# The last attention round in two halves, and ranks of tokens summed by TensorE

## The chip, the cores and the metric

The program runs on one core of one Trainium2 chip. The metric is the device time of one execution in microseconds, as the median of several. Engines: TensorE (PE; its weight loads are listed as PEld), VectorE (DVE), ScalarE (ACT), GpSimd (POOL), and SyncE (SP), which issues loads.

## The reference

Three layers over x, 64 batches of 32 tokens of 256 numbers (2048 tokens, 16 tiles of 128):

```python
x = x + _L0_xattn_ref(ctx_1024, ctx_1024, _layernorm(x), ...)   # attention to 257 context rows per batch
x = x + _L0_attn_ref(_layernorm(x), w_qkv, w_gate, w_out)       # causal linear attention, 16 heads of 64
x = x + _L0_ffn_ref(_layernorm(x), gate_w, w1, w2, w3)          # 8 experts, each token goes to 2

# linear attention
q = jax.nn.elu(q) + 1.0
k = jax.nn.elu(k) + 1.0
k_cum = jnp.cumsum(k, axis=1)
kv = jnp.cumsum(k[..., None, :] * v[..., :, None], axis=1)
numerator = jnp.einsum('bthj,bthij->bthi', q, kv)
denominator = jnp.einsum('bthj,bthj->bth', q, k_cum)
out = numerator / (denominator[..., None] + 1e-06) * gate

# experts
scores = xt @ gate_w.T
top_vals, top_idx = jax.lax.top_k(scores, TOP_K)
top_w = jax.nn.softmax(top_vals, axis=-1)
h = jax.nn.silu(xt @ w1[e].T) * (xt @ w3[e].T);  y = combine * (h @ w2[e].T)
```

## The kernel before

The kernel has four stages. First comes the cross attention, one tile of 128 tokens at a time (`xstep`). Then the linear attention runs in `NR` = 8 rounds of two tiles (`astep`, rounds 0 to 7), written as a pipeline: round r computes q, k, gates and values of its own two tiles and finishes the round before. The two tiles of a round are its halves, s = 0 and 1. Third is the routing: every token chooses two experts, and gets a place in a table of 39 tiles of 128 slots, ordered by expert. Last come the 39 expert tiles (`fstep`), with TensorE busy throughout.

In a round, `a_scores` (L728) makes the scores of a half as 32x32 blocks, 64 matmuls of 64x32. `masks` (L1376) multiplies them on VectorE into `att`, for both halves at once. `a_dens` (L745) sums them into denominators, `den_ev` (L1072) copies these on ScalarE, `recip` (L1393) takes reciprocals on VectorE in pieces of 256, and `norm_att` (L1398) multiplies. `a_nums` (L757) makes the numerators in banks 4 to 7 of PSUM; `gated` (L1405) multiplies by the gates into `goT`; `gated_hi` (L1067, ScalarE) and `gated_lo` (L1415, VectorE) split the result for the three-part product; `a_proj` (`mm3`, L536 to L538) does the output projection, 24 matmuls a half, in bank 6, and `x2` (L1421) adds it to `x_all`. Every engine runs its instructions strictly in the order of its program, and waits on counters (semaphores) stand in front of them.

With the last round (r = 7) the pipeline has to be emptied. `drain` does it, one function on each engine. The finished rounds 0 to 7 are also normalised for the experts (`g_stats`, `g_lns` on VectorE with `g_sqrt` on ScalarE), transposed by TensorE (`g_trs`, L813), copied by ScalarE (`g_xT_ev`, L1096) and multiplied with the gate weights (`g_logits`, L823). Of the logits VectorE takes the two best experts of each token (`top_two`, in three parts: tiles 0 to 5, 6 to 11, 12 to 15), and marks them in `chosen` and, both together, in `both` (128 x 16 tiles x 8 experts). The place of a token within its expert is the number of marks ahead of it. Over the tiles this is a running sum on VectorE in `scan` (`counts`, four doubling steps over the first 12 tiles, and four single steps behind the last part). Within a tile it is a product with a strictly triangular matrix; `ranks` (L833 to L835) does both in three matmuls. VectorE reads their result first in `places` (L1523). `warm(n)` (L829) is n matmuls of 256 columns whose result nobody reads; `warm(6)` stands ahead of `ranks` and `warm(20)` behind it. In the table of slots, TensorE's 32 matmuls of L886 follow, as soon as `in_slot` is there.

SyncE loads the weights of the experts (8 of 2 MB) once the gates and values of round 7 are done. The loads keep the DMA full until shortly before 429 us.

Of the kernel before, what the change touches and what calls it, by code (L numbers as in the profile page):

```python
# [104 lines left out]
def build(nc, ctx, a, out):  # L105
# [116 lines left out]
    scan = [nc.alloc_sbuf_tensor_at(f"scan{i}", [P, NT + 8, E], F32, offset=at["low"] + i * 4 * (NT + 8) * E) for i in range(2)]  # L222
# [15 lines left out]
    LOGIT_BANK = (2, 3, 4)  # L238
# [18 lines left out]
    both = place("both", [P, NT, E])  # L257
# [43 lines left out]
    def sem(name):  # L301
# [29 lines left out]
        "part", "var", "sq", "rs", "ln", "tr", "xT", "mm", "sc", "max", "idx", "keep"))  # L331
    r_step, r_d, r_e1, r_both, r_rank, r_id, r_what, r_in, r_rows, r_tab, r_map, r_done, r_w = (
# [200 lines left out]
    def _(pe):  # L533
# [186 lines left out]
        def a_scores(r, s):  # L720
            wait(pe, a_qku, 8 * r + 8)
            wait(pe, a_o, 8 * r)
            for c in range(FC):
                for b in range(BT):
                    tok = slice(s * P + b * T, s * P + (b + 1) * T)
                    for h in range(2):
                        rows = slice(h * HD, (h + 1) * HD)
                        m = pe.matmul(ps[b * T:(b + 1) * T, 4 + h, (s * FC + c) * T:(s * FC + c + 1) * T],  # L728
                                      kT[rows, c, tok], qT[rows, c, tok], start=True, stop=True,
                                      tile_position=(h * HD, b * T))  # L730
            if s == 1:
                m.then_inc(a_sc, 1)
# [9 lines left out]
        def a_dens(r):  # L742
            wait(pe, a_att, 2 * r + 2)
            for s in range(2):
                pe.matmul(ps[:, 4 + s, :], con[:, C_TWOS:C_TWOS + P], att[:, s, :, :, :].rearrange("p c h t -> p (c h t)"),  # L745
                          start=True, stop=True).then_inc(a_den, 1)

        def a_nums(r, s):
            wait(pe, a_norm, 2 * r + s + 1)
            wait(pe, a_x2, r)  # L750
            wait(pe, a_vu, 4 * r + 4)
            wait(pe, a_o, 8 * r + 4 * s)
            for c in range(FC):
                for h in range(2):
                    for b in range(BT):
                        rows = slice(b * T, (b + 1) * T)
                        m = pe.matmul(ps[h * HD:(h + 1) * HD, 4 + b, (s * FC + c) * T:(s * FC + c + 1) * T],  # L757
                                      v_sb[rows, s, (2 * c + h) * HD:(2 * c + h + 1) * HD], att[rows, s, c, h, :],
                                      start=True, stop=True, tile_position=(b * T, h * HD))
            m.then_inc(a_num, 1)  # L760

        def a_proj(r, u, s, cs=range(FC)):
            wait(pe, a_o, 8 * r + 8)
# [3 lines left out]
            for c in cs:  # L767
                m = mm3(ps[:, 6, s * D:(s + 1) * D], goh[:, c, rows], gol[:, u, c, rows], w_out_hi[:, c, :], w_out_lo[:, c, :],
                        c == 0, c == FC - 1)
# [3 lines left out]
        def astep(r, u):  # L773
# [9 lines left out]
            if r == NR - 1:  # L783
# [5 lines left out]
                a_values(r, 1, range(1, 2))  # L789
                a_gates(r, range(3, 4))  # L790
# [16 lines left out]
        def g_trs(r):  # L807
            wait(pe, g_ln, 2 * r + 2)
            wait(pe, a_gtu, 2 * NT)
            wait(pe, g_xT, r - 1)  # L810
# [6 lines left out]
        def g_logits(r):  # L817
            wait(pe, g_xT, r + 1)
            bank = LOGIT_BANK[part_of(2 * r)]
# [11 lines left out]
        def ranks():  # L831
            pe.wait_ge(r_both, 1)
            pe.matmul(ps[:, 0, 0:NT * E], con[:, C_LOW:C_LOW + P], both[:, :, :].rearrange("p t e -> p (t e)"), start=True, stop=False)  # L833
            pe.matmul(ps[:, 0, 0:NT * E], ones, scan[0][:, 7:7 + NT, :].rearrange("p t e -> p (t e)"), start=False, stop=True)
            pe.matmul(ps[:, 1, 0:E], ones, scan[0][:, 7 + NT, :], start=True, stop=True).then_inc(r_rank, 1)  # L835

        def drain(r, u):
            a_proj(r - 1, 1 - u, 0, range(0, FC // 2))
            a_dens(r)
            a_proj(r - 1, 1 - u, 0, range(FC // 2, FC))  # L840
            a_proj(r - 1, 1 - u, 1)
            g_trs(0)
            g_trs(1)
            g_logits(0)
            a_nums(r, 0)
            g_trs(2)
            g_logits(1)
# [14 lines left out]
            warm(6)  # L862
            ranks()
# [97 lines left out]
    def _(act):  # L961
# [107 lines left out]
        def den_ev(r):  # L1069
            for s in range(2):  # L1070
                wait(act, a_den, 2 * r + s + 1)
                act.activation(den[:, s, :], ps[:, 4 + s, :], ACT.Identity, bias=con[:, C_EPS2:C_EPS2 + 1]).then_inc(a_de, 1)  # L1072
# [25 lines left out]
        def astep(r, u):  # L1098
            before = valid(r - 1, NR)
            if before:  # L1100
                elu_parts(r, range(0, 4))
                den_ev(r - 1)
# [6 lines left out]
            if r == NR - 1:  # L1109
                gates(r, u, range(3, 4))  # L1110
# [7 lines left out]
        def drain(r, u):  # L1118
            den_ev(r)
            for k in range(3):  # L1120
                g_xT_ev(k)
            gated_hi(r, u, 0)
            gated_hi(r, u, 1)
            g_xT_ev(3)
            g_sqrt(r - 1)
            g_xT_ev(4)
            g_xT_ev(5)
# [104 lines left out]
    def _(dve):  # L1232
# [145 lines left out]

        def elu(r, n):
# [38 lines left out]
        def x2(r):  # L1418
            rows = x_all[:, bass.ds(2 * r, 2), :].rearrange("p a d -> p (a d)")
            wait(dve, a_y, r + 1)  # L1420
            dve.tensor_tensor(rows, ps[:, 6, :], rows, ALU.add).then_inc(a_x2, 1)  # L1421
# [30 lines left out]
        def astep(r, u):  # L1452
# [20 lines left out]
            if before:  # L1473
                for s in range(2):
                    gated(r - 1, 1 - u, s)
                    gated_lo(r - 1, 1 - u, s)
# [19 lines left out]
        def top_two(part):  # L1496
            ts = slice(*PARTS[part])
# [18 lines left out]
            link(dve.tensor_tensor(both[:, ts, :], by_k[:, :, 0, :], by_k[:, :, 1, :], ALU.add))  # L1516

        def places():
            dve.wait_ge(r_rank, 1)
            seen = ps[:, 0, 0:NT * E].rearrange("p (t e) -> p t e", e=E)  # L1520
# [20 lines left out]
        def counts():  # L1541
            for b in scan:
                link(dve.memset(b[:, 0:8, :], 0.0))
            link(dve.tensor_copy(scan[0][:, 8:8 + LATE_T, :], both[:, 0:LATE_T, :]))
            cur = 0
            for d in (1, 2, 4, 8):
                link(dve.tensor_tensor(scan[1 - cur][:, 8:8 + LATE_T, :], scan[cur][:, 8:8 + LATE_T, :],
                                       scan[cur][:, 8 - d:8 - d + LATE_T, :], ALU.add))
                cur = 1 - cur
            assert cur == 0  # L1550
# [57 lines left out]
        for t in range(LATE_T, NT - 1):  # L1608
            link(dve.tensor_tensor(scan[0][:, 8 + t, :], scan[0][:, 7 + t, :], both[:, t, :], ALU.add))
        dve.tensor_tensor(scan[0][:, 7 + NT, :], scan[0][:, 6 + NT, :], both[:, NT - 1, :], ALU.add).then_inc(r_both, 1)  # L1610
# [8 lines left out]
        link(dve.tensor_tensor(cmp[:, :, :], ps[:, 1, 0:E].rearrange("p (e a) -> p e a", a=1).to_broadcast([P, E, MAXT]),  # L1619
# [140 lines left out]
```

## Time and profile before

| | us |
|---|---|
| median of 3 runs | 834.27 |
| lowest, highest | 832.51, 835.47 |
| the profiled execution | 833.98 |
| its span in the trace | 832.1 |
| TensorE busy in the span | 796.2 (96%) |
| VectorE busy | 637.9 (77%) |
| ScalarE busy | 564.5 (68%) |
| mean granted TensorE clock | 0.981 |

Times in the trace count from the start of the span. A granted clock of 1.00 is 2.4 GHz, of 0.50 1.2 GHz. The cross attention ends near 105 us, the rounds near 385, and the expert tiles begin at 446.5. The records of successive matmuls overlap, so the distance between two starts tells the pace, not the length of one record. An idle time in brackets is that of the engine just before the row, with what released it.

### The profile page before, as it was taken

The numbers are of one execution on the slowest core, as the hardware profiler recorded it, in microseconds if no ns is written. First come the engines' busy times: TensorE is split into PE (matmuls) and PEld (weight loads), VectorE is DVE, ScalarE is ACT, GpSimd is POOL, SyncE is SP. The second block draws the span as 40 slices with busy tenths as digits, with TensorE's granted clock in tenths as the row PEclk, the third lists the DMA queues.
The fourth block names the chain that finished last, engine by engine and source line by source line (L and its number), as shares of the span: only waits on it lengthen the run. The fifth ranks groups of instructions, "written<-read, shape, count | busy, mean of one in ns | idle before, by whom it ended". The sixth has DMA issues, their size and how long they took to land.

```text
span 832.1 us, 24093 instructions
## 1 busy us (share of the span) xinstructions
PE 796.2 (96%) x9270; PEld 695.7 (84%) x9270; DVE 637.9 (77%) x1033; ACT 564.5 (68%) x879; POOL 281.5 (34%) x190
## 2 busy tenths in 40 slices
PE   6899999999999999999898999999999999999993
PEld 4566588998999999997886889888898888998883
DVE  4444543756758485676679999999999999999992
ACT  3545456554646656463147999989998999999971
POOL 0333375020220202010001545555564555555531
PEclk9999999999999999999689999999999999999997
DMA  9999920000000000005962455445555455544552
GB/s 350 416 417 414 387 79 2 2 16 16 15 28 3 28 2 28 17 15 212 423 241 69 137 147 145 134 126 140 144 147 136 126 137 146 148 136 126 135 143 37
DMA packets 31771, 115.92 MB, mean 139 GB/s; under 512 B 4465, under 2 KB 11570, under 8 KB 26578
## 3 DMA queue, kind: packets, MB, share of 16 engines
q1 hardware_dynamic: 22834, 100.17, 33.5%
q0 software_dynamic: 8864, 14.69, 8.3%
q8 instruction: 57, 0.93, 0.5%
q14 instruction: 16, 0.13, 0.0%
HBM read 105.27 MB, written 9.57 MB: 138 GB/s over the span
## 4 chain that ended last, share of the span: by engine, by line
PE 89%; DVE 4%; DMA 3%; issue 2%; ACT 1%; POOL 0%; POOLq 0%; SPq 0%; DVEq 0%; ACTq 0%
PE ps L536 23%; PE ps L538 22%; PE ps L537 22%; PE ps L941 4%; PE ps L757 3%; PE ps L728 2%; PE ps L589 2%; PE ps L646 2%; PE ps L601 2%; PE ps L623 1%; DMA ctx_t<-in_ctxT 1%; PE ps L904 1%; PE ps L620 1%; PE ps L829 1%; PE ps L823 1%
## 5 line engine op out<-in xcount | busy, mean ns | idle before, releaser
L1599 DVE TENSOR_TENSOR w_lo<-w,w_hi 128x1024 fp32r<-128x1024 f32 x156 | 186.5, 1217 | 0.1
L1163 ACT ACTIVATE w_hi<-w 128x1024 fp32r x156 | 161.3, 1061 | 2.8 <-DVE tile_e L1657 2.8
L522 POOL DMA_INDIRECT out_x<-y_sb,slot_row x39 | 122.5, 3142 | 119.1 <-ACT y_sb L1195 119.1
L536 PE MATMUL ps<-w_hi,xh 128*128 128x512 f32 x312 | 125.7, 403 | 0.4 <-DVE xl L1693 0.4
L538 PE MATMUL ps<-w_hi,xl 128*128 128x512 f32 x312 | 121.9, 391 | 0.0
L537 PE MATMUL ps<-w_lo,xh 128*128 128x512 f32 x312 | 121.6, 390 | 0.0
L536 PE MATMUL ps<-xT_hi,wa_hi 128*128 128x256 f32 x384 | 109.3, 285 | 1.0 <-ACT v_sb L1085 0.8
L537 PE MATMUL ps<-xT_lo,wa_hi 128*128 128x256 f32 x384 | 107.8, 281 | 0.0
L538 PE MATMUL ps<-xT_hi,wa_lo 128*128 128x256 f32 x384 | 107.8, 281 | 0.0
L1174 ACT ACTIVATE w_hi<-w_sb 128x1024 fp32r<-128x1024 f32 x78 | 82.7, 1061 | 29.9 <-DMA w_sb<-in_w 18.3
L510 POOL DMA_INDIRECT xs_sb<-xn_d,slot_row x39 | 68.1, 1746 | 95.9 <-PE ps L904 74.0
L536 PE MATMUL ps<-w_hi,hh 128*128 128x256 f32 x312 | 92.1, 295 | 2.9 <-DVE hl L1700 2.9
L1679 DVE TENSOR_TENSOR w_lo<-w_sb,w_hi 128x1024 fp32r<-128x1024 f32 x78 | 91.8, 1217 | 2.1 <-ACT w_hi L1174 2.1
L538 PE MATMUL ps<-w_hi,hl 128*128 128x256 f32 x312 | 88.8, 285 | 0.0
L537 PE MATMUL ps<-w_lo,hh 128*128 128x256 f32 x312 | 88.7, 284 | 0.0
L536 PEld LDWEIGHTS ps<-xT_hi,wa_hi 128*128 128x128 f32 x384 | 72.3, 188 | 2.2 <-issue 1.2
L537 PEld LDWEIGHTS ps<-xT_lo,wa_hi 128*128 128x128 f32 x384 | 72.4, 188 | 0.4
L538 PEld LDWEIGHTS ps<-xT_hi,wa_lo 128*128 128x128 f32 x384 | 72.3, 188 | 0.0
L1053 ACT ACTIVATE neg<-ps 128x512 f32<-128x512 f32 x64 | 38.2, 597 | 46.9 <-PE ps L538 46.9
L538 PEld LDWEIGHTS ps<-w_hi,xl 128*128 128x128 f32 x312 | 58.6, 188 | 12.8
L536 PEld LDWEIGHTS ps<-w_hi,xh 128*128 128x128 f32 x312 | 58.5, 188 | 12.0 <-DVE xl L1693 0.8
L537 PEld LDWEIGHTS ps<-w_lo,xh 128*128 128x128 f32 x312 | 58.6, 188 | 11.1
(219 smaller groups left out, 1761.4 us busy)
## 6 DMA issues: line engine op xcount, KB each, us to landing
w_sb<-in_w SPq DMA_DIRECT2D x78, 512.0 KB
ctx_t<-in_ctxT SPq DMA_DIRECT2D x16, 1028.0 KB, 8.8
ctx_n<-in_ctxN SPq DMA_DIRECT2D x16, 1024.0 KB
w<-in_w SPq DMA_DIRECT2D x8, 2048.0 KB, 14.3
stage<-in_w_a SPq DMA_DIRECT2D x16, 256.0 KB, 8.5
x_all<-in_x SPq DMA_DIRECT2D x4, 512.0 KB, 8.0
out_x<-x_all POOLq DMA_DIRECT2D x8, 256.0 KB, 3.1
xn_d<-xn_first POOLq DMA_DIRECT2D x6, 256.0 KB, 2.8
```

The source lines that it names most:

```text
L510: pool.indirect_dma_start(xs_sb[:, :], None, xn_d, bass.IndirectOffsetOnAxis(slot_row[:, t:t + 1], 0)).then_inc(f_xs, 16)
L522: pool.indirect_dma_start(out, bass.IndirectOffsetOnAxis(slot_row[:, t:t + 1], 0), y_sb[:, :], None, compute_op=ALU.add).then_inc(f_st, 16)
L536: pe.matmul(dst, l_hi, r_hi, start=first, stop=False)
L537: pe.matmul(dst, l_hi, r_lo, start=False, stop=False)
L538: return pe.matmul(dst, l_lo, r_hi, start=False, stop=last)
L757: m = pe.matmul(ps[h * HD:(h + 1) * HD, 4 + b, (s * FC + c) * T:(s * FC + c + 1) * T], v_sb[rows, s, (2 * c + h) * HD:(2 * c + h + 1) * HD ...
L941: m = pe.transpose(ps[:, 4 + c // 4, (c % 4) * P:(c % 4 + 1) * P], h_sb[:, c * P:(c + 1) * P], ident)
L1053: act.activation(neg[:, n % 2, :], ps[:, n % 4, :], ACT.Relu, scale=-1.0).then_inc(a_neg, 1)
L1163: act.activation(w_hi[:, c, :].rearrange("p (c n) -> p c n", c=DC), w13[:, bass.ds(e, 1), c % 2, :, c // 2 * 512:(c // 2 + 1) * 512].rearr ...
L1174: act.activation(w_hi[:, 4 + c, :], src, ACT.Copy).then_inc(f_dhi, 1)
L1599: dve.tensor_tensor(w_lo[:, c, :].rearrange("p (c n) -> p c n", c=DC), w13[:, bass.ds(e, 1), c % 2, :, c // 2 * 512:(c // 2 + 1) * 512].re ...
L1679: dve.tensor_tensor(w_lo[:, 4 + c, :], src, w_hi[:, 4 + c, :].bitcast(F32), ALU.subtract).then_inc(f_dlo, 1)
```

## The change

It has two parts, both in the emptying of the pipeline. In round 7 every step that took both halves now takes one: masks, densities and their copies. The densities and masks of half 0 move forward, among the gates and values of the round. The numerators of half 0 now stand ahead of the projection of round 6. The densities use banks 0 and 1, the projection of rounds 6 and 7 goes to bank 2, and the logits to banks 3, 6 and 4.

In the routing `scan` and `counts` are gone. `both` has one more tile of zeros. TensorE adds the marks of tile t to all later tiles by products of a matrix of ones with `both`, shifted by d = 1 to 16 tiles, accumulated in bank 7: `ranks_most` for the first 12 tiles after the last logits, `ranks_last` for the last four. Only two `warm` matmuls remain ahead. The last column of eight holds the totals of the experts. `top_two(0)` on VectorE moves behind the statistics of round 7.

```diff
         def a_scores(r, s):
             wait(pe, a_qku, 8 * r + 8)
             wait(pe, a_o, 8 * r)
+            if r == NR - 1 and s == 1:
+                pe.wait_ge(a_att, 2 * r + 2)
...
-            if s == 1:
+            if s == 1 or r == NR - 1:
                 m.then_inc(a_sc, 1)
...
-        def a_dens(r):
-            wait(pe, a_att, 2 * r + 2)
-            for s in range(2):
-                pe.matmul(ps[:, 4 + s, :], con[:, C_TWOS:C_TWOS + P], att[:, s, :, :, :].rearrange("p c h t -> p (c h t)"),
-                          start=True, stop=True).then_inc(a_den, 1)
+        def a_dens(r, s):
+            wait(pe, a_att, 2 * r + 2 * s + 2)
+            wait(pe, a_vu, 4 * r + 2)
+            pe.matmul(ps[:, s, :], con[:, C_TWOS:C_TWOS + P], att[:, s, :, :, :].rearrange("p c h t -> p (c h t)"),
+                      start=True, stop=True).then_inc(a_den, 1)
 
         def a_nums(r, s):
             wait(pe, a_norm, 2 * r + s + 1)
-            wait(pe, a_x2, r)
+            wait(pe, a_x2, r if r < NR - 1 else r - 1)
+            if r == NR - 1:
+                pe.wait_ge(a_att, 2 * r + 4)
...
                 a_values(r, 1, range(1, 2))
+                a_dens(r, 0)
                 a_gates(r, range(3, 4))
                 a_scores(r, 1)
...
+        def summed(d, lo, hi):
+            last = min(NT + 1, hi + d)
+            return pe.matmul(ps[:, 7, (lo + d) * E:last * E], ones, both[:, lo:last - d, :].rearrange("p t e -> p (t e)"),
+                             start=False, stop=hi == NT and d == NT - lo, skip_group_check=True)
+
+        def ranks_most():
+            pe.wait_ge(r_both, 2)
+            pe.matmul(ps[:, 7, 0:(NT + 1) * E], con[:, C_LOW:C_LOW + P], both[:, :, :].rearrange("p t e -> p (t e)"),
+                      start=True, stop=False, skip_group_check=True).then_inc(r_low, 1)
+            for d in range(1, NT + 1):
+                summed(d, 0, LATE_T)
+
+        def ranks_last():
+            pe.wait_ge(r_both, 3)
+            pe.matmul(ps[:, 7, LATE_T * E:NT * E], con[:, C_LOW:C_LOW + P], both[:, LATE_T:NT, :].rearrange("p t e -> p (t e)"),
+                      start=False, stop=False, skip_group_check=True)
+            for d in range(1, NT - LATE_T + 1):
+                m = summed(d, LATE_T, NT)
+            m.then_inc(r_rank, 1)
 
         def drain(r, u):
-            a_proj(r - 1, 1 - u, 0, range(0, FC // 2))
-            a_dens(r)
-            a_proj(r - 1, 1 - u, 0, range(FC // 2, FC))
+            a_dens(r, 1)
+            a_nums(r, 0)
+            a_proj(r - 1, 1 - u, 0)
             a_proj(r - 1, 1 - u, 1)
+            a_nums(r, 1)
             g_trs(0)
             g_trs(1)
+            a_proj(r, u, 0)
             g_logits(0)
-            a_nums(r, 0)
             g_trs(2)
+            a_proj(r, u, 1)
             g_logits(1)
-            a_nums(r, 1)
             g_trs(3)
             g_logits(2)
-            a_proj(r, u, 0)
-            a_proj(r, u, 1)
+            g_trs(4)
             g_logits(3)
-            g_trs(4)
             g_trs(5)
...
-            warm(6)
-            ranks()
+            ranks_most()
+            warm(2)
+            ranks_last()
             warm(20)
...
+        def masks_half(r, s):
+            mask = con[:, C_MASK:C_MASK + T].rearrange("p (a t) -> p a t", a=1).to_broadcast([P, FC, T])
+            wait(dve, a_sc, r + s + 1)
...
-        def counts():
-            for b in scan:
-                link(dve.memset(b[:, 0:8, :], 0.0))
-            link(dve.tensor_copy(scan[0][:, 8:8 + LATE_T, :], both[:, 0:LATE_T, :]))
...
         def drain(r, u):
-            masks(r)
-            g_lns(r - 2)
             recip(r, 0)
             recip(r, 1)
-            x2(r - 1)
             norm_att(r, 0)
+            masks_half(r, 1)
+            g_lns(r - 2)
             recip(r, 2)
             recip(r, 3)
             norm_att(r, 1)
             gated(r, u, 0)
+            x2(r - 1)
             gated_lo(r, u, 0)
             gated(r, u, 1)
             gated_lo(r, u, 1)
             g_stats(r - 1)
-            top_two(0)
             g_lns(r - 1)
             x2(r)
             g_stats(r)
+            top_two(0)
             g_lns(r)
             top_two(1)
-            counts()
+            no_tiles()
```

The order of the instructions on TensorE after the last logits, before:

```order
1960 L823 MATMUL ps<-gw,xT_122 128x8 x4
1961 L829 MATMUL ps<-con 128x256 x6
1962 L833 MATMUL ps<-both,con 128x128
1963 L834 MATMUL ps<-scan_126,con 128x128
1964 L835 MATMUL ps<-scan_126,con 128x8
1965 L829 MATMUL ps<-con 128x256 x20
```

and of the changed kernel, where L850 is the line of `summed` and L846 that of `warm`:

```order
1962 L840 MATMUL ps<-gw,xT_122 128x8 x4
1963 L855 MATMUL ps<-both,con 128x136
1964 L850 MATMUL ps<-both,con 128x96 x5
1965 L850 MATMUL ps<-both,con 128x88
...
1975 L850 MATMUL ps<-both,con 128x8
1976 L846 MATMUL ps<-con 128x256 x2
1977 L862 MATMUL ps<-both,con 128x32
1978 L850 MATMUL ps<-both,con 128x32
1979 L850 MATMUL ps<-both,con 128x24
1980 L850 MATMUL ps<-both,con 128x16
1981 L850 MATMUL ps<-both,con 128x8
1982 L846 MATMUL ps<-con 128x256 x20
```

Three matmuls have become 17 ahead of the two `warm` and five behind them.

VectorE at the end of round 7 and the start of `drain`, before (goT is `gated` of round 6, att<-ps,con the masks, den the reciprocals):

```order
376 L1405 SCALAR_TENSOR_TENSOR goT<-goT,ps 128x8x32 x4
377 L1415 TENSOR_TENSOR gol<-goT,goh 128x4x128 x2
378 L1238 BN_STATS bn_2_52<-x_all 128x6 x2
...
385 L1376 TENSOR_TENSOR att<-ps,con 128x16x32 x2
386 L1445 RECIPROCAL rstd_135<-rstd_135 128x2
387 L1449 TENSOR_SCALAR xn_first<-x_all,mean_131,rstd_135 128x256 x2
388 L1393 RECIPROCAL den<-den 128x256 x2
389 L1421 TENSOR_TENSOR x_all<-ps,x_all 128x512
390 L1398 TENSOR_TENSOR att<-att,den 128x512
```

and of the changed kernel:

```order
376 L1445 SCALAR_TENSOR_TENSOR goT<-goT,ps 128x8x32 x4
377 L1416 TENSOR_TENSOR att<-ps,con 128x8x32 x2
378 L1455 TENSOR_TENSOR gol<-goT,goh 128x4x128 x2
379 L1271 BN_STATS bn_2_52<-x_all 128x6 x2
...
386 L1433 RECIPROCAL den<-den 128x256 x2
387 L1438 TENSOR_TENSOR att<-att,den 128x512
388 L1416 TENSOR_TENSOR att<-ps,con 128x8x32 x2
389 L1485 RECIPROCAL rstd_133<-rstd_133 128x2
390 L1489 TENSOR_SCALAR xn_first<-x_all,mean_129,rstd_133 128x256 x2
391 L1433 RECIPROCAL den<-den 128x256 x2
```

The masks of half 0 have moved up behind `gated`, and those of half 1 stand behind two reciprocals and the normalisation of half 0.

## Rows read from the trace of the kernel before

**Rows 1.** Stages: length, busy time of PE, PEld, DVE, ACT, POOL; PEclk, DMA share, GB/s

```profile
392.80:397.40 4.60, 4.35 (x155) 4.05 (x153) 4.36 (x4) 1.26 (x3) 0.71 (x1) 1.00 1.03 439
397.40:406.30 8.90, 5.66 (x146) 5.40 (x146) 5.15 (x13) 2.46 (x5) 0.00 (x0) 0.50 0.99 420
406.30:411.10 4.80, 4.80 (x23) 4.80 (x24) 4.53 (x32) 1.04 (x3) 0.00 (x0) 0.51 1.03 434
411.10:414.10 3.00, 3.00 (x28) 3.00 (x27) 0.99 (x4) 0.00 (x0) 0.71 (x1) 1.00 1.02 426
414.10:421.30 7.20, 6.26 (x56) 5.79 (x54) 5.41 (x35) 3.01 (x6) 1.43 (x2) 1.00 0.99 364
421.30:428.10 6.80, 6.80 (x21) 5.72 (x22) 4.76 (x34) 0.95 (x2) 0.00 (x0) 0.50 1.00 419
```

**Rows 2.** Timeline, 377 to 392: start, length, engine, line, work, idle before

```profile
377.56 1.33 PE L728 MATMUL ps<-qT,kT 64*32 64x32 f32 x128
380.72 0.16 DVE L1439 TENSOR_SCALAR mean<-mean 128x2 f32<-128x2 f32 x1
381.27 0.36 PE L536 MATMUL ps<-xT_hi,wa_hi 128*128 128x256 f32 x1 [0.78 <-ACT v_sb L1085]
385.07 0.28 PE L728 MATMUL ps<-qT,kT 64*32 64x32 f32 x11 [0.97 <-issue]
385.42 1.29 DVE L1376 TENSOR_TENSOR att<-ps,con 128x512 f32<-128x512 f32 x2 [4.54 <-PE ps L728]
386.80 1.95 PE L745 MATMUL ps<-att,con 128*128 128x512 f32 x4
388.65 3.37 DVE L1393 RECIPROCAL den<-den 128x256 f32<-128x256 f32 x2 [1.02 <-ACT den L1072]
```

**Rows 3.** Timeline, numerators of half 0 of round 7

```profile
395.11 1.49 PE L757 MATMUL ps<-att,v_sb 32*64 32x32 f32 x128
```

**Rows 4.** Timeline, projection of round 6 at full clock

```profile
390.02 0.28 PE L536 MATMUL ps<-w_out_hi,goh 128*128 128x256 f32 x1
390.37 0.28 PE L536 MATMUL ps<-w_out_hi,goh 128*128 128x256 f32 x1
```

**Rows 5.** Timeline, weight loads of logits at half and at full clock, and transposes

```profile
404.55 1.83 PEld L823 LDWEIGHTS ps<-gw,xT 128*128 128x128 f32 x8
414.06 0.98 PEld L823 LDWEIGHTS ps<-gw,xT 128*128 128x128 f32 x8
414.99 1.07 PE L813 MATMUL ps<-con,xn_first 128*128 128x128 f32 x8
```

**Rows 6.** Timeline of the routing, from the first part of the top two

```profile
408.75 0.20 DVE L1501 COPY sc<-ps 128x48 f32<-128x48 f32 x1
410.98 0.21 DVE L1516 TENSOR_TENSOR both<-chosen 128x48 f32<-128x48 f32 x1
420.78 1.45 PE L823 MATMUL ps<-gw,xT 128*128 128x8 f32 x8 [0.69 <-ACT xT L1096]
421.79 1.13 DVE L1547 TENSOR_TENSOR scan<-scan 128x96 f32<-128x96 f32 x4
423.22 0.19 DVE L1501 COPY sc<-ps 128x32 f32<-128x32 f32 x1
425.10 0.19 DVE L1516 TENSOR_TENSOR both<-chosen 128x32 f32<-128x32 f32 x1
425.32 0.57 DVE L1609 TENSOR_TENSOR scan<-scan,both 128x8 f32<-128x8 f32 x3
428.30 8.23 PE L829 MATMUL ps<-con 128*128 128x256 f32 x37
```

**Rows 7.** Chain of waits from 400 to 429, then timeline of the table's matmuls

```profile
400.48 1.83 issue
422.23 5.32 PE ps L829 x12
428.55 0.30 DVE prod L1523
437.02 0.66 PE L886 MATMUL ps<-what_id,in_slot 128*128 128x40 f16 x20
438.01 0.87 PE L886 MATMUL ps<-what_id,in_slot 128*128 128x40 f16 x12 [0.33 <-DVE in_slot L1536]
```

More of the change, by code:

```diff
@@ L256, in build @@
     chosen = place("chosen", [P, NT * TOP, E])
-    both = place("both", [P, NT, E])
+    both = place("both", [P, NT + 1, E])
     tiles = [place(f"tiles{i}", [P, 4 + E]) for i in range(2)]
@@ L762, in a_proj @@
         def a_proj(r, u, s, cs=range(FC)):
-            wait(pe, a_o, 8 * r + 8)
+            if r < NR - 1:
+                wait(pe, a_o, 8 * r + 8)
+            if r == NR - 2:
+                wait(pe, a_vu, 4 * (NR - 1) + 3)
+            if r == NR - 1:
+                wait(pe, a_x2, r)
             wait(pe, a_gl, 4 * r + 2 * s + 2)
@@ L809, in g_trs @@
             wait(pe, a_gtu, 2 * NT)
+            wait(pe, a_de, NT)
             wait(pe, g_xT, r - 1)
@@ L818, in g_logits @@
             wait(pe, g_xT, r + 1)
+            if part_of(2 * r):
+                wait(pe, a_o, 8 * NR)
             bank = LOGIT_BANK[part_of(2 * r)]
@@ L1067, in gated_hi, with den_ev @@
                 act.activation(goh[:, cs, rows], goT[:, u, cs, rows], ACT.Copy).then_inc(a_gh, 1)
[L1069 to L1072, printed above, removed]
+        def den_ev(r, s):
+            wait(act, a_den, 2 * r + s + 1)
+            act.activation(den[:, s, :], ps[:, (s if r == NR - 1 else 4 + s), :], ACT.Identity,
+                           bias=con[:, C_EPS2:C_EPS2 + 1]).then_inc(a_de, 1)
         def gates(r, u, ns=range(4)):
@@ L1101, in astep @@
                 elu_parts(r, range(0, 4))
-                den_ev(r - 1)
+                for s in range(2):
+                    den_ev(r - 1, s)
             elu_parts(r, range(4 if before else 6, 8))
@@ L1118, in drain @@
         def drain(r, u):
-            den_ev(r)
-            for k in range(3):
-                g_xT_ev(k)
[L1122 to L1127, printed above, removed]
+            den_ev(r, 1)
+            gated_hi(r, u, 0)
+            g_xT_ev(0)
+            g_xT_ev(1)
+            gated_hi(r, u, 1)
+            g_xT_ev(2)
+            g_sqrt(r - 1)
+            for k in range(3, 6):
+                g_xT_ev(k)
             g_sqrt(r)
@@ L1377, in masks @@
                                   ALU.mult).then_inc(a_att, 1)
+        def masks_half(r, s):
+            mask = con[:, C_MASK:C_MASK + T].rearrange("p (a t) -> p a t", a=1).to_broadcast([P, FC, T])
+            wait(dve, a_sc, r + s + 1)
+            for h in range(2):
+                dve.tensor_tensor(att[:, s, :, h, :], ps[:, 4 + h, s * FC * T:(s + 1) * FC * T].rearrange("p (c t) -> p c t", t=T), mask,
+                                  ALU.mult).then_inc(a_att, 1)
         def elu(r, n):
@@ L1475, in astep @@
                     gated(r - 1, 1 - u, s)
+                    if r == NR - 1 and s == 1:
+                        masks_half(r, 0)
                     gated_lo(r - 1, 1 - u, s)
@@ L1496, in top_two @@
         def top_two(part):
+            if part == 0:
+                link(dve.memset(both[:, LATE_T:, :], 0.0))
             ts = slice(*PARTS[part])
@@ L1539, in in_slots, with no_tiles @@
                                   ALU.is_equal).then_inc(r_in, 1)
-        def counts():
-            for b in scan:
-                link(dve.memset(b[:, 0:8, :], 0.0))
-            link(dve.tensor_copy(scan[0][:, 8:8 + LATE_T, :], both[:, 0:LATE_T, :]))
[L1545 to L1550, printed above, removed]
+        def no_tiles():
             for b in tiles:
```

27 lines of the change are left out of this document (12 added, 15 removed).

## The prediction

> **What bounds the kernel now.** I read three views in this order: stages of the last attention round and of the routing, with engines and granted clock [rows 1]; the timeline of single steps there [rows 2 to 6]; the chain of waits at the end of the stretch [rows 7]. TensorE has something to do nearly all the time, but from 397.4 to 411 and from 421.3 to 428.1 it runs at half clock, 1.2 GHz (granted 0.50) in place of 2.4 [rows 1]. Ahead of the first fall it did logits, small numerators and transposes (392.8 to 397.4); ahead of the second, transposes and logits with short waits (414.1 to 421.3). It rose after dense work: output projections from 406.3, or `warm` matmuls from 422.2 [rows 1, 7]. Everything up to the scores of round 7 and everything after VectorE reads the ranks at 428.55 [rows 7] stays as it is, so the change is worth the shift of that 428.55, plus what the `warm(20)` behind it does. The profiled execution took 833.98 us, 0.29 us under the median, and the sum is made against it. About 0.3%, 2.5 us, can be told from no change.
>
> **Paces.** A projection matmul takes 0.117 us at full clock (three from 390.02 to 390.37 [rows 4]) and 0.21 at half (23 in 4.80 us, 406.3 to 411.1 [rows 1]). A small fp32 matmul is two passes, each paced by its weight load: 8 loads in 0.98 us, 0.12 each, at full clock, and 8 in 1.83 us, 0.23 each, at half [rows 5]. A `warm` matmul is two passes: 12 in 5.32 us gives 0.43 each at half clock [rows 7], so 0.22 at full.
>
> **Part 1, up to the end of the scores: no gain, no loss.** The densities of half 0 (0.87 us, half of the four passes that took 386.8 to 388.5 [rows 2]) stand on TensorE ahead of the last gates, where it waited 0.78 us for v_sb [rows 2]. That hides all but 0.1 us. On VectorE the mask of half 0 waits for the scores that end at 378.9 and costs some 0.8 us (two of 128x256, a bit over half of the 1.29 us of the two full ones); what ended at 380.88 now ends at 382.4 [rows 2]. The scores of half 1 still end at 385.4, with their instruction wait of nearly 1 us included [rows 2].
>
> **Part 2, a new idle stretch.** TensorE's next instruction is the densities of half 1, and they need its masks. VectorE has two reciprocals (3.37 us [rows 2]) from 382.4 to 385.8, the normalisation (0.6) and then the masks (0.8): 387.2. TensorE idles from 385.4 to 387.2; before, it had output projections there. Queued behind that wait are the numerators and all 48 projection matmuls of round 6, so nothing fills it.
>
> **Part 3, the two chains.** From 387.25 at full clock: densities 0.87, numerators 1.42 (128 passes, 1.49 with the tail [rows 3]), 48 projections 5.6, numerators 1.42, eight transposes 1.05 [rows 5], 24 projections 2.8, logits and a transposition of half a round 1.45, 24 projections 2.8. End: 404.6. VectorE keeps up: its reciprocals for half 1 lie at 389.2 to 392.5 beside the projections, the low parts of half 0 are there at 397.4 (needed 397.6) and of half 1 at 400.7 (needed 401.9). Before, the last projection ended at 414.1 [rows 1]: 9.5 us gained. What is behind it grows, since more logits were pushed to the end: seven of 0.96, five transpositions of 0.5, and some 0.8 of waiting for the last copy by ScalarE: 10.0 us, end 414.6, in place of 422.2 (420.78 and 1.45 [rows 6]). VectorE's `top_two(0)` (408.75 to 411.2, 2.4 us [rows 6]) moves behind the statistics of round 7; there ScalarE's square root stands behind its fifth copy until 409.9, so it costs nothing. Without that cover it would be 2.1 us. **Balance 7.6 us gained.**
>
> **Part 4, the ranks.** VectorE loses the scan (1.13 us and its clears, from 421.2 to 422.9) and four small additions (0.76) [rows 6]. But TensorE gets 17 matmuls in place of `warm(6)`: 34 passes; then `warm(2)`; then 5 matmuls, 10 passes. It starts on them only when the last logits are through, and VectorE's marks need just 2.1 us more (423.22 to 425.29 [rows 6]), so TensorE's own length decides: at full clock 34 x 0.12 = 4.1, 0.9, 1.2, and 0.25 to VectorE: 6.4 us, as long as now (422.2 to 428.55, with the low clock in it). At half clock 34 x 0.23 = 7.8, 1.7, 2.3, 0.25: 12.05 us, **5.6 us more**. The trace has no such matmul; the lower bound is 0.03 a pass (f16, 20 in 0.66 us [rows 7]), which would take 3.8 us off the sum at full clock and some 7 at half, before VectorE's marks decide; the upper one is the 0.23 above. I take the fp32 loads, since both operands are fp32.
>
> **Part 5, the clock.** The rows show falls after work much like what the change puts in two places. First, scores (64x32 tiles, as small as the numerators before 397.4), a wait for instructions and 1.8 us of idleness: I expect a fall between 385.5 and 388.5. Then densities and numerators cost up to 0.87 and 0.65 more, and the clock rises after 4.8 us of projections, as from 406.3 [rows 1], or up to a third sooner: 16 to 24 matmuls that are each 0.092 slower: 1.5 to 2.2. Together 2.4 to 3.7; I take **3.1 us**. Second, 10 us of nothing but transposes and logits before the ranks, longer than the 7.2 us after which the clock fell at 421.3. The ranks are small matmuls, and between 397.4 and 406.3 small ones gave no rise. So they run at half clock. And `warm(20)` begins at half clock, where now it begins at full (428.3 [rows 6]): with a rise after about 4.5 us, a little sooner than from 406.3, it ends 2.25 us later. The 32 table matmuls behind it start at 437.02 and wait for VectorE's in_slot at the end (0.33 us and the last four [rows 7]), which leaves 0.65 us of slack, so **1.6 us** comes through.
>
> The rule of the Trainium skill speaks against this fall: "TensorE: Matmul & The Clock Gate", section "Why this matters for your kernels", ties the drop in mid-kernel to an idle gap between bursts, and advises against long ones alone. The fall at 397.4 came with TensorE recorded busy for 4.35 of 4.60 us [rows 1], so by the trace light work is enough; by the page the clock would stay full (first rival).
>
> **Sum.** -7.6 (halves) + 0 (DVE steps, covered by TensorE's) + 5.6 (ranks at half clock) + 3.1 (fall at the idle stretch) + 1.6 (`warm(20)`) = +2.7. 833.98 + 2.7 = **836.7 us**.
>
> **Rivals.**
> - Clock full throughout: -7.6 + 0 = 826.4. For it: at 414.1 to 421.3 seven light microseconds passed at full clock. Against: the fall at 397.4. Chance 0.08.
> - It falls at the idle stretch, and is up again and stays full through the ranks: -7.6 + 3.1 = 829.5. Not slower, and decided by whether the fall comes after the ranks' first pass. Chance 0.18.
> - No fall at the idle stretch, but one before the ranks: -7.6 + 5.6 + 1.6 = -0.4, 833.6. Chance 0.15.
> - **Slower side**: the second fall comes early among the final transposes and logits (within 5 us of 404.6). Then these take their half-clock pace, 1.83 for logits in place of 0.98 [rows 5], and four of each still to come cost 3.3 more: 840.0. It decides from the third logits on. Chance 0.16.
> - Numerators of half 0 now follow the scores of half 1 with two matmuls between: 512 short instructions. The waits for instructions that stood in the scores (1 us) and numerators (1.83 us [rows 7]) come back as one more, of up to 2 us, while the expert weights fill the DMA (share 0.96 to 1.03 [rows 1]): 838.7. Chance 0.05.
> - Forecast: 0.38.
>
> **Numbers.** Forecast's own range 835.0 to 838.2 (3.1 may be 2.4 to 3.7, 1.6 may be 0.6 to 2.5). Leaving out the first rival and the upper half of the slower one: 828.5 to 840.0. Faster by over 0.3%: the first two and a small part of the third, 0.29. Within: the rest of the third, half of the forecast: 0.33. Slower: 0.38.
>
> **What would show it.** Right: TensorE idle for about 1.8 us before the densities of half 1; granted clock 0.50 some time between 386 and 395; last projection of round 7 done at 405 to 409; the 34 passes of the first ranks in 7 to 8 us; `warm(20)` over 10 us in place of 8.2. Wrong: 34 passes in about 4 us with granted clock 1.00, or passes far under 0.12; a last projection before 405 (no first fall); VectorE, not TensorE, the last before it reads the ranks. The loads of the experts go on to the same time near 428.8 (DMA share 1.00 to 428.1 [rows 1]), since bandwidth holds them; were they to end after ScalarE wants w13, some 12 us behind the ranks, that would cap any gain over 12 us, which no case reaches.

## The result, and the profile after

The changed kernel took 842.9 us (median of 10 executions, 837.9 to 846.3), the kernel before beside it 835.6 us (832.5 to 837.6). The ratio is 1.009, 95% interval 1.007 to 1.011, so it is slower by 0.9%. A second set of executions gave 841.0 us and 1.006 (1.004 to 1.008). The forecast was 836.7 us, with a range from 828.5 to 840.0: the side was right, the size too small, and the time lies above the range. The profiled execution took 837.87 us (span 836.0, 3.9 more than before) and is the fastest of its ten, so part of the miss does not show in its trace.

First the stages between changes of the clock (columns as in [rows 1]):

```profile
387.67:397.91 10.24, 7.30 (x148) 6.04 (x147) 5.84 (x9) 0.69 (x1) 0.71 (x1) 0.50 0.99 419
397.91:418.39 20.48, 20.44 (x296) 20.03 (x294) 13.51 (x72) 6.75 (x13) 2.85 (x4) 1.00 1.01 428
418.39:435.45 17.06, 16.41 (x65) 15.33 (x66) 6.58 (x43) 3.54 (x8) 0.00 (x0) 0.50 0.56 233
```

The clock is at 1.2 GHz for 10.2 and 17.1 us, where it was for 13.7 and 6.8 us before [rows 1].

Then the timeline of the changed kernel, end of the round. The rows answer to [rows 2, 3]; L751 is densities, L765 numerators, L1461 `x2`, the first row the scores of half 1.

```profile
384.95 0.29 PE L734 MATMUL ps<-qT,kT 64*32 64x32 f32 x14 [0.81 <-issue]
386.37 0.75 DVE L1416 TENSOR_TENSOR att<-ps,con 128x256 f32<-128x256 f32 x2
387.18 1.63 PE L751 MATMUL ps<-att,con 128*128 128x512 f32 x2 [1.94 <-DVE att L1416]
388.73 1.82 PE L765 MATMUL ps<-att,v_sb 32*64 32x32 f32 x111
393.49 0.52 PE L765 MATMUL ps<-att,v_sb 32*64 32x32 f32 x17 [2.94 <-issue]
411.03 0.69 DVE L1461 TENSOR_TENSOR x_all<-ps,x_all 128x512 f32<-128x512 f32 x1 [1.00 <-PE ps L542]
```

The idle time ahead of the densities is there (1.94 us), and the clock falls half a microsecond after it. What the forecast's sum doesn't have is the fifth row: after 111 of 128 numerators TensorE stands for 2.94 us, and neither data nor an engine released it ("issue").

The routing, which answers to [rows 6, 7]; L855 and L862 are the products with the triangular matrix, L850 those with ones, L846 `warm`, L1569 the first reading of the ranks:

```profile
419.04 1.87 PE L840 MATMUL ps<-gw,xT 128*128 128x8 f32 x8 [0.69 <-ACT xT L1127]
420.77 0.80 PE L855 MATMUL ps<-both,con 128*128 128x136 f32 x2
421.36 6.83 PE L850 MATMUL ps<-both,con 128*128 128x96 f32 x32
422.98 0.19 DVE L1562 TENSOR_TENSOR both<-chosen 128x32 f32<-128x32 f32 x1
428.05 2.05 PE L846 MATMUL ps<-con 128*128 128x256 f32 x4
429.89 0.47 PE L862 MATMUL ps<-both,con 128*128 128x32 f32 x2
430.18 1.85 PE L850 MATMUL ps<-both,con 128*128 128x32 f32 x8
431.89 10.63 PE L846 MATMUL ps<-con 128*128 128x256 f32 x40
432.14 0.61 DVE L1569 TENSOR_TENSOR prod<-chosen,ps 128x128 f32<-128x128 f32 x2 [8.17 <-PE ps L850]
442.36 0.97 PE L917 MATMUL ps<-what_id,in_slot 128*128 128x40 f16 x32
```

The marks are complete at 423.2. VectorE then waits 8.17 us for products whose operands are all there, and it reads at 432.14 in place of 428.55 [rows 7]. TensorE has no gap in this stretch; it is its own length that decides, 0.21 us for each fp32 pass. The columns do not show in it: the 26 passes with 96 to 32 columns take 0.21 us each (421.36 to 426.77), and so do the last six with 24 to 8 (426.77 to 428.05).

### The profile page after: what moved, and what is told of

The parts are those of the page before. It is cut to its first block, busy times and chain, and to the rows that moved or that the text cites. A ratio compares the mean times of both kernels' runs of the same rounds, so it can differ in the third digit from the quotient of the medians.

```text
span 836.0 us, 24160 instructions
## 1 busy us (share of the span) xinstructions
PE 802.4 (96%) x9300; PEld 702.2 (84%) x9300; DVE 635.9 (76%) x1025; ACT 565.8 (68%) x879; POOL 284.3 (34%) x190
## 4 chain that ended last, share of the span: by engine, by line
PE 92%; DVE 2%; issue 2%; ACT 1%; DMA 1%; POOL 0%; POOLq 0%; SPq 0%; DVEq 0%; ACTq 0%
PE ps L540 23%; PE ps L542 22%; PE ps L541 22%; PE ps L972 4%; PE ps L765 3%; PE ps L734 2%; PE ps L593 2%; PE ps L846 2%; PE ps L650 2%; PE ps L605 2%; PE ps L627 1%; PE ps L935 1%; PE ps L850 1%; PE ps L840 1%; PE ps L624 1%
## 5 line engine op out<-in xcount | busy, mean ns | idle before, releaser
L526 POOL DMA_INDIRECT out_x<-y_sb,slot_row x39 | 125.3, 3213 | 116.3 <-ACT y_sb L1228 116.3
```

The source lines that it names most:

```text
L526: pool.indirect_dma_start(out, bass.IndirectOffsetOnAxis(slot_row[:, t:t + 1], 0), y_sb[:, :], None, compute_op=ALU.add).then_inc(f_st, 16)
```

## The experiments

Two explanations were on record at the start: that the fp32 passes of the ranks at half clock cost the time, or that the two halves did, through the new idle time and the wait in the numerators. The first batch takes the change apart.

**The changed kernel once more.**

> The changed kernel, nothing altered, for a second profile: ten executions lay between 837.9 and 846.3 us, and the profiled one was the fastest. Theory A (the granted clock, which falls at a place that differs between executions): 843 us again, and a profile over 840 us shows a longer stretch at 0.50, with waits for instructions as in the first profile (0.81 and 2.94 us). Theory B (waits for instructions): the same time, but the profile shows these waits grown to 5 to 8 us together, with the clock low for about as long as in the first one (10.2 and 17.1 us).

Measured: 841.0 us, ratio 1.006 (1.004 to 1.008). The wait in the numerators is there again, and VectorE reads the ranks at 433.49:

```profile
395.23 0.35 PE L765 MATMUL ps<-att,v_sb 32*64 32x32 f32 x17 [2.34 <-issue]
```

The profiled execution took 841.45 us, 3.6 more than the other, and neither theory has the reason. The waits have not grown (0.55 and 2.34 us), and the time at 0.50 between 385 and 437 is 23.9 us, less than the 27.3 of the first profile. The section on the hardware comes back to that.

**The ranks alone:** kernel before, with its old `drain`, but the sums of marks on TensorE.

```diff
-            warm(6)
-            ranks()
+            ranks_most()
+            warm(2)
+            ranks_last()
             warm(20)
...
-            counts()
+            no_tiles()
```

> The kernel before with the second part of the change alone: marks of tiles summed on TensorE (44 passes, two warm matmuls ahead of the last ten) in place of VectorE's scan, the last round as it was. Theory A: the last logits end at about 422 us, the clock is at 0.50 there, and VectorE reads the ranks 11.2 us later as in the first profile of the changed kernel, not 6.4: 4.9 us slower, and 0.3 more behind warm(20), so 840.5 us (838 to 842). Theory B: the passes are no longer than the warm matmuls that they replace, the loss of 7 us sits in the halves: 836 us or less.

Measured: 842.6 us, ratio 1.007 (1.004 to 1.009), 6.9 us slower than before. Timeline of the routing in this kernel, where L833 is the products with ones and L829 `warm`:

```profile
423.04 1.21 PE L823 MATMUL ps<-gw,xT 128*128 128x8 f32 x8 [0.69 <-ACT xT L1111]
424.69 6.83 PE L833 MATMUL ps<-both,con 128*128 128x96 f32 x32
435.22 11.66 PE L829 MATMUL ps<-con 128*128 128x256 f32 x40
435.48 0.61 DVE L1542 TENSOR_TENSOR prod<-chosen,ps 128x128 f32<-128x128 f32 x2 [8.26 <-PE ps L833]
446.72 0.96 PE L901 MATMUL ps<-what_id,in_slot 128*128 128x40 f16 x32
```

From the end of the last logits (424.25) to VectorE's reading it is 11.2 us, against 6.3 before. `warm(20)` takes 11.66 us for its 40 passes; the row of [rows 6] has only 37 of them, and all 40 took 8.88 us before. So this part alone gives the whole loss.

**The halves alone:** the changed kernel, with `scan`, `counts` and `warm(6)` as before (the diff above the other way round).

> The changed kernel with VectorE's scan, six warm matmuls and three matmuls for the ranks as before; the two chains of the last round stay. Theory A: the halves bring 1.3 us up to the last logits in an execution like the first profile (420.9 in place of 422.2): 834.5 us, and up to 836 in the median. Theory B: most of the loss is here, since the 512 short instructions of scores and numerators stand in a row: 840 us or more, with waits for instructions of 3 us and more in the profile.

Measured: 835.3 us beside 835.7, ratio 0.9995 (0.998 to 1.001): no change to be told. The timeline shows where the expected gain went:

```profile
390.11 1.82 PE L765 MATMUL ps<-att,v_sb 32*64 32x32 f32 x111
394.15 0.52 PE L765 MATMUL ps<-att,v_sb 32*64 32x32 f32 x17 [2.21 <-issue]
412.38 0.95 PE L840 MATMUL ps<-gw,xT 128*128 128x8 f32 x8
428.36 0.61 DVE L1550 TENSOR_TENSOR prod<-chosen,ps 128x128 f32<-128x128 f32 x2 [1.65 <-PE ps L852]
```

It went to the wait for instructions (2.21 us) and to a clock at half from 386.87 to 400.53. TensorE worked 10.21 us in that stretch; by halving, which is an estimate, that costs 5.1 us, where the forecast's sum had 3.1. So the logits behind the last projection start at 412.38, against 414.18 before, only 1.8 us sooner. The longer light stretch takes that back (last logits to 422.1 against 422.2), and the ranks are read at 428.36 against 428.55. The explanation that puts the loss in the halves has fallen: they lose nothing. But they gain nothing either.

**The projection first:** the changed kernel, with work that is ready ahead of the wait for the masks.

```diff
         def drain(r, u):
+            a_proj(r - 1, 1 - u, 0)
             a_dens(r, 1)
             a_nums(r, 0)
-            a_proj(r - 1, 1 - u, 0)
             a_proj(r - 1, 1 - u, 1)
```

> The changed kernel with one block moved: the 24 projection matmuls of half 0 of round 6 stand ahead of the densities of half 1, where TensorE was idle from 385.2 to 387.2, instead of behind the numerators. Both theories expect a gain. Theory A: no idle stretch, granted clock 1.00 through 386 to 398, last projection at about 406 in place of 410.8: 838 us (4 to 5 less than the changed kernel). Theory B: the wait of 2.94 us in the numerators goes, since 48 instructions of 5.6 us in place of 2 stand between scores and numerators, whether the clock falls or not: 838 to 840 us with the clock low in 388 to 398 all the same.

Measured: 839.6 us, ratio 1.004 (1.003 to 1.006), 1.4 us less than the changed kernel beside it, where 4 to 5 were expected; the intervals of the two ratios overlap, so a gain is not shown.

```profile
390.28 1.09 PE L765 MATMUL ps<-att,v_sb 32*64 32x32 f32 x86
394.39 0.68 PE L765 MATMUL ps<-att,v_sb 32*64 32x32 f32 x42 [3.02 <-issue]
```

The idle time ahead of the densities is gone, but the wait for instructions stays, 3.02 us. It stands behind 86 numerators in place of 111, 25 sooner, where 24 matmuls were put ahead: the same place in the row of instructions. And it ends at nearly the same time, 394.39. In the four profiles so far the next instructions come between 393.5 and 395.3, whatever TensorE does before.

**Ranks in f16.** The marks are 0 or 1 and the matrices 0 or 1, so f16 holds them exactly, and the sums stay in fp32 in PSUM.

```diff
-    both = place("both", [P, NT + 1, E])
+    both = place("both", [P, NT + 1, E], F16)
+    low_h = nc.alloc_sbuf_tensor_at("low_h", [P, P], F16, offset=gol_at + 4096)
+    ones_h = nc.alloc_sbuf_tensor_at("ones_h", [P, P], F16, offset=gol_at + 4096 + 256)
...
+                link(dve.tensor_copy(low_h[:, :], con[:, C_LOW:C_LOW + P]))
+                link(dve.tensor_copy(ones_h[:, :], ones))
```

The matmuls of the ranks take `ones_h` and `low_h` in place of the fp32 matrices.

> The changed kernel with the marks, the matrix of ones and the triangular one in f16, so that each of the 22 rank matmuls is one pass instead of two and loads f16 weights. The sums are the same whole numbers. Theory A (length of TensorE's passes at half clock): 34 and 10 passes of 0.21 us become 17 and 5 of 0.03 to 0.07; VectorE's marks decide, and it reads the ranks about 3.5 us behind the last logits instead of 11.2. warm(20) starts at half clock and gives 1 us back: 7 us off the changed kernel, 835 us. Theory B (what costs is only the low clock that the change brings in, whatever the passes are): the clock is as low as before, and less than 2 us come off: 840 us.

Measured: 832.3 us, ratio 0.996 (0.994 to 0.998): 8.7 us less than the changed kernel's second set (each of the two was set against executions of the kernel before, which agree within 0.1 us), and faster than the kernel before.

```profile
424.79 1.07 PE L852 MATMUL ps<-both,ones_h 128*128 128x96 f16 x16
425.71 2.05 PE L848 MATMUL ps<-con 128*128 128x256 f32 x4
427.01 0.19 DVE L1566 TENSOR_TENSOR both<-chosen 128x32 f16<-128x32 f32 x1
427.63 0.24 PE L852 MATMUL ps<-both,ones_h 128*128 128x32 f16 x4
428.04 0.61 DVE L1573 TENSOR_TENSOR prod<-chosen,ps 128x128 f32<-128x128 f32 x2
```

16 passes in 1.07 us in place of 32 in 6.83, at the same half clock. Now the last marks decide (complete at 427.20), and VectorE reads the ranks 0.84 us behind them.

**The ranks alone, in f16:** both edits on the kernel before.

> The kernel before with the second part of the change alone, in f16. With fp32 it was 842.6 us. Theory A: the same gain as in the changed kernel, 8 us at most: VectorE reads the ranks about 3 us behind the last logits (422.2), 425.5 in place of 428.55 before, and warm(20) at half clock takes 1 to 1.5 us back: 834 us, 1 to 2 us under the kernel before. Theory B: 840 us.

Measured: 834.5 us, ratio 0.998 (0.996 to 1.000), 8.1 us less than the ranks alone in fp32, and not to be told from the kernel before. With the old order of the round, too, the type of the operands decides. Both operands changed type at once, so which of them sets the pace is not shown.

**The loads later.** The wait for instructions was suspected to stem from the DMA, which the expert weights fill. Here the first five of these loads wait until the numerators of half 0 are through.

```diff
+        sp.wait_ge(a_num, NT - 1)
```

> The changed kernel, where the first five loads of expert weights wait for the numerators of half 0 of round 7. Theory A (the block of 16 KB of instructions that TensorE waits for stands in the DMA behind the expert loads; in six profiles it moves at 391 to 393, 8.2 to 8.7 us after the one ahead of it, whatever TensorE does): with the DMA empty from 383 to 390 the wait of 2.94 us in the numerators goes, down to 1 us or none. Theory B (TensorE asks for its next block only when it runs out): the wait stays at 2 to 3 us. The loads then end about 436 instead of 428.8, still ahead of their use at 445, so the time follows the wait: 840 us by A, 843 by B.

Measured: 840.5 us, ratio 1.005 (1.003 to 1.007).

```profile
388.45 1.98 PE L752 MATMUL ps<-att,con 128*128 128x512 f32 x2 [2.21 <-DVE att L1417]
390.36 2.02 PE L766 MATMUL ps<-att,v_sb 32*64 32x32 f32 x128
429.66 0.61 DVE L1570 TENSOR_TENSOR prod<-chosen,ps 128x128 f32<-128x128 f32 x2 [8.17 <-PE ps L851]
```

The DMA is nearly empty from 383 to 390 (share 0.02), all 128 numerators run in one piece, and the ranks are read 2.5 us sooner than in the changed kernel. In this profile the wait went with the loads. The clock is low for 3.4 us in place of 10.2, but in the second profile of the changed kernel it was low for two times 3.4 us, so this need not be the loads' doing. The median is only 0.5 us lower than that of the changed kernel's second set, within the noise of the two, so a gain in time is not shown.

**`warm(8)` ahead of the ranks,** to have them at full clock.

```diff
+            warm(8)
             ranks_most()
```

> The changed kernel with eight warm matmuls ahead of the first rank matmul, to see what the rank passes take with the clock at 2.4 GHz. Theory A: the warm matmuls (16 passes, up to 6.9 us) bring the clock up; the 34 passes then take 4.1 us (0.12 each) in place of 6.9 to 7.3, warm(2) 0.9, the last ten 1.2, so VectorE reads the ranks 12 to 13.5 us behind the last logits instead of 11.2, and warm(20) is short again (8.7 us): 843 us, 0 to 2 over the changed kernel. Theory B (a pass of this shape takes 0.21 us whatever the clock): 15 to 18 us behind the last logits, and 847 us.

Measured: 842.4 us, ratio 1.008 (1.005 to 1.012).

```profile
421.31 5.81 PE L846 MATMUL ps<-con 128*128 128x256 f32 x16
427.19 3.63 PE L850 MATMUL ps<-both,con 128*128 128x96 f32 x32
431.76 1.04 PE L850 MATMUL ps<-both,con 128*128 128x32 f32 x8
432.91 0.61 DVE L1570 TENSOR_TENSOR prod<-chosen,ps 128x128 f32<-128x128 f32 x2 [4.46 <-PE ps L850]
```

The same 32 passes take 3.63 us at full clock, 0.11 each. But the `warm` matmuls that raise the clock take 5.8 us, a little over the 5.3 that the passes and the second `warm` then save, and VectorE reads 11.5 us behind the last logits, as without them.

**The best of both:** projection first, ranks in f16.

> The changed kernel with both edits, the projection ahead of the densities of half 1 and the rank matmuls in f16. The projection took 1.4 to 3.3 us off the changed kernel, f16 should take 7: theory A 832 us, 3 to 4 us under the kernel before. Theory B: 837 us.

Measured: **831.2 us**, ratio 0.994 (0.992 to 0.996), the fastest median of the study. The wait in the numerators is still 3.47 us. After the last logits (end 424.0) the ranks are read at 427.17:

```profile
422.13 1.87 PE L842 MATMUL ps<-gw,xT 128*128 128x8 f32 x8 [0.69 <-ACT xT L1129]
427.17 0.61 DVE L1573 TENSOR_TENSOR prod<-chosen,ps 128x128 f32<-128x128 f32 x2
```

**Halves with the projection first, `scan` as before.**

> The first part of the change alone (VectorE's scan, six warm and three rank matmuls as in the kernel before), with the projection of half 0 of round 6 ahead of the densities of half 1. The halves alone gave 835.3, the same as before; the projection took 1.4 to 3.3 us off the changed kernel. Theory A (idle stretch and clock are what takes the gain of the halves away): 833 us. Theory B (only the wait for instructions does, and that stays 3 us here): 835 us.

Measured: 832.7 us, ratio 0.997 (0.995 to 0.999). Without the idle time the halves do gain, about 2.7 us, although the wait for instructions is 3.21 us here. The clock is low for 6.8 us (394.56 to 401.38), against 13.7 in the halves alone, so the idle time and the clock are what took the gain, as theory A had it. The kernel with the f16 ranks as well was 1.6 us lower still, in another set.

**The last projection later,** to break the light stretch up (`a_proj(7, 1)` behind three logits in place of one), and the same with the loads later:

```diff
-            a_proj(r, u, 1)
             g_logits(1)
             g_trs(3)
             g_logits(2)
+            a_proj(r, u, 1)
```

> The fastest so far (projection ahead, f16 ranks, 831.15 us), with the last projection of round 7 moved behind three logits instead of one, so that what follows it is 7.6 us of transposes and logits instead of 10. Theory A (the clock falls in that stretch in each profile, 3 to 8 us behind its start): in some executions it now falls only at the ranks, VectorE reads them 1 to 3 us sooner: 829.5 us. Theory B (only TensorE's sum counts, and it is the same): 831 us. A third outcome: the statistics of the last tiles come too late for the last transposes, and it is 1 us slower.

> The same, and the first five loads of expert weights wait for the numerators of half 0. Theory A: the wait for instructions of 3 us goes, 2 to 3 us less: 827.5 us. Against it: the loads end about 436, and ScalarE wants the last weights at 438 to 440, so they just pass; if they end later, the time is no better than without.

Measured: 832.1 us, ratio 0.996 (0.994 to 0.999), and 834.3 us, 0.998 (0.996 to 1.000). The first is no better than 831.2: the clock still fell at 411.6 and 421.9, and the third outcome came too, a wait for the statistics of the last tiles:

```profile
422.51 1.11 PE L830 MATMUL ps<-con,xn_last 128*128 128x128 f32 x4 [1.58 <-DVE xn_last L1491]
```

In the second the wait in the numerators is 1.00 us, and the ranks are read at 420.59, 6.6 us sooner than in the best kernel. But the loads, begun later, now end too late for ScalarE, which waits 8.73 us for the experts' weights:

```profile
420.59 0.61 DVE L1574 TENSOR_TENSOR prod<-chosen,ps 128x128 f32<-128x128 f32 x2
438.95 3.90 ACT L1199 ACTIVATE w_hi<-w 128x1024 fp32r x4 [8.73 <-DMA w<-in_w]
```

This is the cap that the forecast named in its last paragraph, met by loads that begin later and ranks that come 8 us sooner than before the change.

## Where the prediction was right and where it failed

**Part 1 held.** The masks of half 0 fit, and in the profiled execution the scores of half 1 end at 385.24 (forecast 385.4).

**Part 2 held.** Idle 1.94 us to 387.18 (forecast 1.8, to 387.2).

**Part 3, the step that failed.** The last projection was to end at 404.6, or at 407.7 with the fall of the clock. The logits behind it start at 410.83, 3.1 us later. 2.94 of these are the wait for instructions in the numerators of half 0, which the sum has at nothing. The prediction had it as a rival with a chance of 0.05 and at most 2 us; it stood in every profile that kept the halves and the old start of the loads, with 2.2 to 3.5 us. The reading that misled was of [rows 7]: before, a wait of 1.83 us stood at 400.48, and I took it as something that moves with the numerators and may come back. It does not move with the numerators. Counted from the end of the short wait in the scores to the next wait, the trace has exactly 256 recorded instructions of TensorE, weight loads and matmuls together. It is so in all ten profiles where the halves run into such a wait, with 111 numerators or with 24 projections and 86 numerators. In the three profiles with the old order it is 512, two such blocks, and in the kernel before the wait there is the 1.83 us of [rows 7]:

```profile
402.31 1.62 PE L757 MATMUL ps<-att,v_sb 32*64 32x32 f32 x96 [1.83 <-issue]
```

The traces also record the DMA packets that bring instructions, blocks of 16 KB. Once the expert loads fill the DMA, the next block comes 8.2 to 9.0 us after the last: it starts at 390.94 in the kernel before, at 391.01 in the changed one and at 393.02 in its second set. In the two profiles of the changed kernel TensorE goes on 2.5 and 2.2 us behind that start, and in the kernel before it goes on at 402.31, 2.4 us behind the block at 399.92. So the wait is for a block of 256 instructions. Before, TensorE had worked through its block only at about 395.5, and the one of 390.94 was there; the halves want it at 390.6, some 5 us sooner. With the loads where they were, the part of the gain that lies ahead of about 393.5 could not be had.

**Part 3, behind it.** Light stretch 10.1 us from the first logits to the end of the last (forecast 10.0), no cost on VectorE for `top_two(0)`: held.

**Part 4 held.** 11.2 us from the last logits to VectorE (forecast 12.05): the passes take 0.21 rather than 0.23. That the fp32 operands are the price, and TensorE's own length what decides, is shown by the ranks in f16. The fp32 passes came near the upper bound; f16 has half as many, 0.07 us each, and took off 8.1 and 8.7 us.

**Part 5.** The fall at the idle stretch came (387.67) and so did the one in the light stretch (418.39). There the Trainium skill ("TensorE: Matmul & The Clock Gate", section "Why this matters for your kernels") names an idle gap as what drops the clock; the second fall came in logits and transposes, with TensorE recorded busy for 20.44 of the 20.48 us ahead of it (second row of the first fence), so for such work the measurement decides. The fall at the idle stretch was too small in the sum: by halving (an estimate), the 7.30 us worked in it cost 3.7 us and the 10.21 us in the halves alone 5.1, where the sum has 3.1. `warm(20)` took 10.63 us as forecast ("over 10"), but the 8.2 us set against it is a row with 37 of the 40 passes; all took 8.88 us, so it grew by 1.75. Only 0.35 us of that came through in place of 1.6: from VectorE's reading to the end of the tables' preparation it is 11.79 us (432.14 to 443.93) against 11.44 (428.55 to 439.99). So the slack was 1.4 us and not the 0.65 that I read from the matmuls of the table. The kernel with the ranks alone says the same: `warm(20)` grew by 2.8 us there, and 1.4 came through.

The sum in the trace, forecast and measured:

| | forecast | measured |
|---|---|---|
| last projection, with the first fall | -6.4 | -3.3 |
| longer light stretch behind it | +1.9 | +2.0 |
| ranks | +5.6 | +4.9 |
| `warm(20)` | +1.6 | +0.35 |
| together | +2.7 | +3.9 |

**On medians** the ranks with `warm(20)` were to cost 7.2 us and cost 6.9 (ranks alone). The halves with their fall were to gain 4.5 and gained 0.4 (halves alone, the interval includes 0). This is the wrong term: 4.1 us. The profile of the halves alone has its two parts, 2.2 us for the wait for instructions, which the sum had at nothing, and 2.0 more for the fall of the clock (estimated above). The distance of 6.2 us from 836.7 to 842.9 is 1.6 of level (the kernel before had 835.57 in that set, and the sum began at 833.98), 4.1 for the halves, 0.3 less for the ranks, and 0.8 that the two parts together cost more than one by one (7.3 against 6.5), which is less than the 1.9 us between the two sets of the changed kernel.

**The range** ended at 840.0 because the wait for instructions was a rival by itself and not a term beside the others: with 3 us more on the slower rival it would have ended at 843.

## What to carry to other kernels

Moving a sum from VectorE to TensorE is paid by the number of matmuls and the type of the operands, at the clock that this stretch will have, and not by the columns as long as these are few (8 to 96 here). 22 small fp32 matmuls cost 7 us here; in f16, which holds such small whole numbers exactly, that loss was gone. When a change brings code forward, look at when its instructions themselves arrive, and whether bulk loads are running then; small matmuls use up a block of 256 instructions in a few microseconds. And put ready work, not a wait, behind the last scores: with the ranks as before, one line moved took the halves from no gain to 2.7 us. In the two pairs with the new ranks it was worth 1.4 and 1.1 us, within the noise.

## What was not expected of the hardware

A block of instructions came 8.2 to 9.0 us after the last one while the expert loads filled the DMA (share 0.99), and 6.0 and 5.9 us in the two kernels with later loads. TensorE waited for it 2.2 to 3.5 us in every profile with the halves and the old start of the loads, and 0 and 1.00 us in those two kernels. That bulk loads slow it rests on these two profiles.

The clock falls at other places in each execution of the same program: in the changed kernel at 387.67 and 418.39 in one profile, at 389.19, 396.02 and 419.91 in another. Behind the table's preparation the first took 392.1 us to the end and the second 394.1, with the same instructions. By halving (an estimate), the low clock in that part costs 6.8 us in the first and 7.8 in the second; this is one of the 2 us, and the other is not explained.

The executions of the changed kernel spread over 8 us (837.9 to 846.3), those of the kernel before over 5. The record has the mean granted clock of each execution, profiled or not, and it goes with the time: from 0.979 at 838.98 us to 0.971 at 846.34, with a correlation of -0.84 in the first set of the changed kernel and -0.75 in the second. A mean clock lower by 0.008 is worth 6.8 us of 844 (an estimate), against 7.4 between these two, so most of the spread is time at half clock. The same holds between the kernels: in the second set the median clock is 0.975 for the changed kernel and 0.982 for the one before, worth 5.9 us where 5.2 were measured. With the ranks in f16 it is 0.982 again. What makes the clock fall earlier in one execution than in another stays open. The two profiles of the changed kernel, with 0.977 and 0.978, are a pair that it doesn't tell apart: of the 3.6 us between them, 1.4 have arisen before VectorE reads the ranks, and most of the rest in the experts.
